# Linear attention scores from fp16 halves of phi, as 64-row products that alternate between row halves

## What is computed

```python
# layer 1, linear attention, per token s of each sequence b (16 heads of 64)
h = _ln(x, g1, beta1)
q = _phi((h @ wq).reshape(b, s, H, DH), proj)     # phi(y) = elu(y @ proj) + 1
k = _phi((h @ wk).reshape(b, s, H, DH), proj)
v = (h @ wv).reshape(b, s, H, DH)
kv = kv + k_t[..., :, None] * v_t[..., None, :]   # a running sum over the tokens
ksum = ksum + k_t
num = jnp.einsum('bhd,bhde->bhe', q_t, kv)
den = jnp.einsum('bhd,bhd->bh', q_t, ksum) + 1e-06
outs = num / den[..., None]
x = x + outs.reshape(b, s, H * DH) @ wo
x = x + (gelu(_ln(x, g2, beta2) @ w1 + b1) @ w2 + b2)
```

## Time and profile before

| | |
|---|---|
| median of 3 runs | 2643.98 us (2643.9 to 2645.58) |
| span of the profiled execution | 2644.0 us |
| layer 1 in it | about 0 to 853 us |
| first scores of group 0, 3 and 4 | 80.07, 276.90 and 375.74 us |
| PE, DVE, ACT, POOL busy share of the span | 93%, 71%, 60%, 26% |

### The profile page before, as it was taken

One profiled execution on the slowest core, in us unless ns is written; L12 is line 12 of the kernel. 1 busy time (PEld: TensorE's weight loads), 2 busy tenths in 40 slices (PEclk: granted clock), 3 DMA queues, 4 the chain that ended last, 5 costly groups with the idle time before them and its releaser, 6 DMA issues. The chain is left out here.

```text
span 2644.0 us, 61265 instructions
## 1 busy us (share of the span) xinstructions
PE 2451.5 (93%) x20194; PEld 1852.6 (70%) x20194; DVE 1877.7 (71%) x4914; ACT 1595.1 (60%) x3456; POOL 678.1 (26%) x1179
## 2 busy tenths in 40 slices
PE   5998998999996699999999999999999999979997
PEld 3775875875875467777777777777777777667886
DVE  5656656656654588778777887788777878656657
ACT  4335235235231578777777877787777778634444
POOL 1000100100101343434344443444343444200003
PEclk7999999999998799999999999999999999958999
DMA  4000000000000200000000000000000000022201
GB/s 127 27 1 1 0 0 0 0 0 0 0 1 5 86 14 9 13 8 13 8 13 8 13 8 13 8 13 8 13 7 12 8 7 0 2 65 77 92 24 56
DMA packets 45652, 50.08 MB, mean 19 GB/s; under 512 B 19120, under 2 KB 37664, under 8 KB 45504
## 3 DMA queue, kind: packets, MB, share of 16 engines
q1 hardware_dynamic: 45504, 48.45, 6.2%
HBM read 44.78 MB, written 3.67 MB: 18 GB/s over the span
## 5 line engine op out<-in xcount | busy, mean ns | idle before, releaser
L1390 POOL TENSOR_SCALAR p_norm<-p,p_rec 112x375 f32<-112x375 f32 x512 | 303.7, 593 | 831.6 <-DVE p_rec L1232 676.8
L1114 ACT ACTIVATE p<-s_neg,neg_max 112x375 f32<-112x375 f32 x512 | 309.8, 605 | 110.4 <-DVE neg_max L1227 88.0
L1236 DVE TENSOR_TENSOR pt_lo<-b_t,pt_hi 125x336 f16<-125x336 f32 x512 | 259.4, 507 | 158.4 <-ACT pt_hi L1120 148.1
L1212 DVE SCALAR_TENSOR_TENSOR k<-b_pb,k 64x375 f16<-64x375 f32 x512 | 280.9, 549 | 38.7 <-ACT k L1105 28.6
L1008 PE MATMUL b_t<-ident,p_norm 112*125 112x112 f32 x1536 | 283.1, 293 | 3.0 <-POOL p_norm L1390 3.0
L1105 ACT ACTIVATE k<-b_pb 64x375 f16<-64x375 f32 x512 | 244.9, 478 | 60.4 <-PE b_pb L64 53.8
L62 PE MATMUL b_o<-pt_hi,v_hi 125*64 125x112 f16 x1536 | 273.5, 221 | 6.2 <-DVE b_o_lo L1241 5.2
L1227 DVE CUSTOM_DVE_ANT_0 s_neg<-b_s,mask_bias 112x375 f32<-112x375 f32 x512 | 275.7, 539 | 0.6 <-ACT p L1114 0.4
L62 PEld LDWEIGHTS b_o<-pt_hi,v_hi 125*64 125x64 f16 x1536 | 167.5, 109 | 149.5 <-issue 103.0
L1120 ACT ACTIVATE pt_hi<-b_t 125x336 f16<-125x336 f32 x512 | 227.0, 443 | 61.5 <-PE b_t L1008 39.1
L63 PE MATMUL b_o<-pt_lo,v_hi 125*64 125x112 f16 x1536 | 261.3, 213 | 0.0
(11 more groups left out here) (247 smaller groups left out, 7003.8 us busy)
## 6 DMA issues: line engine op xcount, KB each, us to landing
w_raw<-in_L_ffn_W_dram SPq DMA_DIRECT2D x16, 1024.0 KB, 7.4
ctx<-in_ctx_dram SPq DMA_DIRECT2D x32, 375.0 KB
out_dram<-c_z SPq DMA_DIRECT2D x8, 448.0 KB, 3.2
x_sb<-in_x_dram SPq DMA_DIRECT2D x1, 3136.0 KB, 19.2
ff<-in_L_attn_w_dram SPq DMA_DIRECT2D x2, 1024.0 KB, 6.7
b_stage<-in_L_xattn_Wkv_dram SPq DMA_DIRECT2D x2, 1024.0 KB, 9.9
mask<-in_mask_BxS_bf_dram SPq DMA_DIRECT2D x32, 41.0 KB, 2.6
a_raw<-in_L_attn_wq_dram SPq DMA_DIRECT2D x1, 1024.0 KB, 5.0
```

Of the source, the lines that this page charges most:

```text
L1114: act.activation(p32[:, h % 4, :], s_neg[:, h % 2, :], ACT.Exp, bias=neg_max[:, h % 4:h % 4 + 1], scale=-1.0, accum_out=p_sum[:, h % 4:h % ...
L1212: ins = dve.scalar_tensor_tensor(k2[half_rows[1 - r], par, h, 0:S2], ps[rows, 0:S2], UNSCALE, k2[rows, par, h, 0:S2], ALU.mult, ALU.subtract)
L1236: dve.tensor_tensor(pt_lo[:, h % 4, :], t_ps[h % 2][0:JP, 0:JT * T], pt_hi[:, h % 4, :], ALU.subtract).then_inc(pt_lo_done, 1)
L1390: pool.tensor_scalar(p_norm[:, h % 4, :], p32[:, h % 4, :], p_rec[:, h % 4:h % 4 + 1], 0.0, ALU.mult, ALU.add).then_inc(p_norm_done, 1)
```

## The change

1. phi goes first to a ring of four fp32 tiles, `phi32`, by one 128-row VectorE operation for Q and K alike; VectorE then copies it to fp16 (`q_hi`, `k_hi`), and GpSimd subtracts to get the low half (`q_lo`, `k_lo`; new function `phi_low`). VectorE waits for its own first operation ahead of the copy, and for GpSimd's low half of four tiles before.
2. `kz`, its zeroes and the memset are gone.
3. `scores` forms two units at once, on even steps only: the even heads of four tiles go to `s_ps[0]` and the odd heads to `s_ps[1]`, three 64-row fp16 products for each head, in turn on rows 0 to 63 and 64 to 127. It waits for all masks before t.
4. `turn_output` makes four transposes on odd steps instead of two on each; `o32` interleaves the two units of a pair.

```diff
-        qt = sb("qt", [P, KI, GT], F32)
-        kz = sb("kz", [P, H, GT], F32)
+        NR = 4
+        phi32 = sb("phi32", [P, NR, GT], F32)
+        q_hi, q_lo, k_hi, k_lo = (sb(f"a_{n}", [P, KI, GT], F16) for n in ("q_hi", "q_lo", "k_hi", "k_lo"))
...
             def scores(g, u):
-                b, quad = divmod(u, 4)
-                at_least(pe, s_masked, UNITS * g + u - 1)
+
+                b, first = u // 4, 2 * (u % 4)
+                if b == 0:
+                    pe.wait_ge(qk_lo_done, tile_count(g, "K", first + 3) + 1)
+                at_least(pe, s_masked, UNITS * g + u)
+                cols = slice(b * T, (b + 1) * T)
                 for i in range(4):
-                    h = 4 * quad + i
-                    mm = pe.matmul(s_ps[u % 2][0:T, i * T:(i + 1) * T], kz[:, h, b * T:(b + 1) * T],
-                                   qt[:, h // 2, b * T:(b + 1) * T], start=True, stop=True)
-                mm.then_inc(s_ready, 1)
+                    for n, (k, q) in enumerate(((k_hi, q_hi), (k_lo, q_hi), (k_hi, q_lo))):
+                        for r in range(2):
+                            rows = slice(DH * r, DH * (r + 1))
+                            mm = pe.matmul(s_ps[r][0:T, i * T:(i + 1) * T], k[rows, first + i, cols], q[rows, first + i, cols],
+                                           start=(n == 0), stop=(n == 2))
+                            if i == 3 and n == 2:
+                                mm.then_inc(s_ready, 1)
...
             def turn_output(g, u):
                 pe.wait_ge(o_done, UNITS * g + u + 1)
-                ps = claim(use(g, "O", u // 2)) if u % 2 == 0 else bank(use(g, "O", u // 2))
-                for m in range(2):
-                    c = (2 * (u % 2) + m) * T
-                    mm = pe.transpose(ps[:, c:c + T], o32[:, u % 4, m * P:(m + 1) * P], ident[0:T, 0:T])
-                if u % 2 == 1:
-                    mm.then_inc(pb_ready, 1)
+                ps = claim(use(g, "O", u // 2))
+                for m in range(4):
+                    mm = pe.transpose(ps[:, m * T:(m + 1) * T], o32[:, u // 2 % 2, m * P:(m + 1) * P], ident[0:T, 0:T])
+                mm.then_inc(pb_ready, 1)
...
-                written(g, "K", KI)
                 written(g, "V", 2 * G4)
                 for t in range(STEPS):
-                    if t < UNITS:
+                    if t < UNITS and t % 2 == 0:
                         scores(g, t)
                     if VALUES_AT <= t < UNITS + VALUES_AT:
                         values(g, t - VALUES_AT)
-                    if TURN_AT <= t < UNITS + TURN_AT:
+                    if TURN_AT <= t < UNITS + TURN_AT and (t - TURN_AT) % 2 == 1:
                         turn_output(g, t - TURN_AT)
...
             def phi(g, kind, i):
...
-                if kind == "K":
-                    for r in range(2):
-                        rows = slice(DH * r, DH * (r + 1))
-                        ins = dve.scalar_tensor_tensor(kz[rows, 2 * i + r, :], ps[rows, 0:GT], 0.0, phi_exp[rows, i % 2, :],
-                                                       ALU.max, ALU.add)
-                else:
-                    ins = dve.scalar_tensor_tensor(qt[:, i, :], ps[:, 0:GT], 0.0, phi_exp[:, i % 2, :], ALU.max, ALU.add)
-                ins.then_inc(free_of(u), 1)
+                at_least(dve, qk_lo_done, n + 1 - NR)
+                dve.scalar_tensor_tensor(phi32[:, i % NR, :], bank(u)[:, 0:GT], 0.0, phi_exp[:, i % 2, :],
+                                         ALU.max, ALU.add).then_inc(free_of(u), 1)
+                dve.wait_ge(free_of(u), freed(u))
+                dve.tensor_copy(hi[:, i, :], phi32[:, i % NR, :]).then_inc(qk_hi_done, 1)
...
-            dve.wait_ge(kz_zeroed, 1)
...
+            def phi_low(g, kind, tiles):
+                hi, lo = (k_hi, k_lo) if kind == "K" else (q_hi, q_lo)
+                for i in tiles:
+                    settle(pool, passed, (qk_hi_done, tile_count(g, kind, i) + 1))
+                    pool.tensor_tensor(lo[:, i, :], phi32[:, i % NR, :], hi[:, i, :], ALU.subtract).then_inc(qk_lo_done, 1)
...
+                if not is_last(g):
+                    phi_low(g + 1, "Q", range(EARLY))
                 ln_rstd(g, 1)
+                if not is_last(g):
+                    phi_low(g + 1, "Q", range(EARLY, KI))
+                    phi_low(g + 1, "K", range(KI))
...
-            pool.memset(kz[:, :, :], 0.0).then_inc(kz_zeroed, 1)
...
+            for kind in ("Q", "K"):
+                phi_low(0, kind, range(KI))
```

More of the change, by code:

```diff
@@ L127, in layer1 @@
         rec = sb("rec", [T, 2, 4], F32)
-        o32 = sb("o32", [T, 4, 4 * DH], F32)
+        o32 = sb("o32", [T, 2, 8 * DH], F32)
         o_hi, o_lo = (sb(f"o_{n}", [P, 2, KI, T], F16) for n in ("hi", "lo"))
@@ L189, in use, with tile_count @@
             return g, len(PRE) + (LAST if is_last(g) else MAIN).index((kind, i))
+        def tile_count(g, kind, i):
+            return 2 * KI * g + (KI if kind == "K" else 0) + i
         def ready(u):
@@ L220, in layer1 @@
         h_hi_done = [sem(f"a_h_hi_done{i}") for i in range(2)]
-        kz_zeroed, pads_done = sem("a_kz_zeroed"), sem("a_pads_done")
+        qk_hi_done, qk_lo_done, pads_done = sem("a_qk_hi_done"), sem("a_qk_lo_done"), sem("a_pads_done")
         relu_done, exp_done = sem("a_relu_done"), sem("a_exp_done")
@@ L300, in values @@
                     mm = pe.matmul(o_ps[u % 2][0:T, i * (DH + 1):(i + 1) * (DH + 1)], sm[0:T + 1, u % NSM, i * T:(i + 1) * T],
-                                   v1[0:T + 1, b, 4 * quad + i, :], start=True, stop=True)
+                                   v1[0:T + 1, b, head(u, i), :], start=True, stop=True)
                 mm.then_inc(av_done, 1)
@@ L516, in divide @@
                     dve.wait_ge(pb_ready, ready(use(g, "O", u // 2 - 2)))
-                dve.tensor_tensor(o32[:, u % 4, :].rearrange("p (i d) -> p i d", d=DH), ps[:, :, 0:DH],
+                dve.tensor_tensor(o32[:, u // 2 % 2, :].rearrange("p (i r d) -> p i r d", r=2, d=DH)[:, :, u % 2, :], ps[:, :, 0:DH],
                                   rec[:, u % 2, :].unsqueeze(2).to_broadcast([T, 4, DH]), ALU.mult).then_inc(o_done, 1)
```

9 lines of the change are left out of this document (6 added, 3 removed).

## The result

The changed kernel takes 2800.07 us (median of four runs, 2796.03 to 2801.91) against 2644.03 beside it: a ratio of 1.0588, 95% interval 1.0575 to 1.0601. The forecast was 2682, the range 2634 to 2728. The sign was right; the size, 38 us for 156, was not.

A forecast was written before the change was run, and what follows sets the result against it. PE, busy 93% of the span and never pausing in the attention loop, was taken as the bound. 2644.0 + 56 (pairing's wait) - 14 (behind the loop) - 4 (ahead of group 0) = 2682 us, range 2634 to 2728.

The forecast's parts named there:

- S: PE time of a pair's 24 fp16 scores products in the attention loop: 1.2 us, 0.37 less than before.
- rival 1: Both row halves' scores products stream together, S = 0.6: 2648 us, no measurable change; chance 0.22.
- The wait that comes with pairing: Attention loop: a pair's scores wait for the last mask of the pair before; +7.0 us a group, +56 in all.
- my formula: A pair's cycle in the loop: S + 2.86 us, + 0.53 with `o_lo`, + 0.33 for each small even-step operation.
- point (b): PE idle 1.5 to 2 us ahead of each pair's scores, masks waiting for `a_o`; about 35 us to unit 14.
- The loop's end: End of a group's attention loop: as before, fewer transposes being no gain.
- Point (e): PE clock 1.00 in the attention loop; 0.50 would show the clock falling there.
- rival 3: The clock falls in the attention loop, four 3.4 us stretches a group at half clock: +48, sum 2730; chance 0.10.
- layers 2 and 3 start when layer 1 ends: Listed among the other edits, which cost nothing: the layers behind layer 1 add no time.
- phi and the stretch behind the loop: Copies beside POOL's subtractions, 1.35 us a tile, and sums moved off `xh`: -2 us a group, -14 over seven.
- rival 2: The stretch behind the loop gains 5.4 us a group, with the row halves together: 2624 us; chance 0.10.
- Ahead of group 0: `kz` memsets no longer delay `xh`, eight Q tiles take back 1.6: -4 us, bounds -6 and 0.

The follow-up runs named there:

- the unpaired kernel: Changed kernel with each unit's scores issued in its own step as twelve products of one row half, waiting for the mask of two units before: 2780.41 us.
- unpaired, written-out kernel: Changed kernel with scores unpaired and DVE's groups 1 to 6 of layer 1 written out in place of a loop: 2753.47 us.
- filler run: Changed kernel with five fp16 products of 448 columns added ahead of each pair's scores, overwritten by them: 2766.96 us.
- The four buffers: Changed kernel with four buffers for masked scores (sm) instead of two, pairing kept: 2746.15 us.
- 28 waits: Kernel before with 28 long-satisfied waits added in DVE's loop of layer 1, at a group's end: 2653.59 us beside 2641.3.
- moved loops: Changed kernel with satisfied waits added once ahead of layer 1's loop, 170 on DVE and 240 on PE, no loop altered: 2782.12 us.
- the run with the sums later: Kernel before with one more wait: POOL's two sums of a group wait for DVE's four xh of the second layer norm: 2599.9 us.
- run without low halves: Changed kernel with POOL's subtraction of the low halves replaced by a memset of two columns from group 1 on: 2749.28 us.
- fillers and four buffers: Changed kernel, still paired, with four sm buffers, DVE's groups written out and five 448-column products ahead of each pair's scores: 2728.02 us.

## Why the prediction missed

Step by step, in the order in which it put them.

*S.* Taken as 1.2 us a pair, measured 0.61: the forecast took the serial pace, and rival 1 (both halves stream at once) was right. With it my sum would have been 2648, further off and no measurable change, so that the sign came out right owes something to a wrong S. The Trainium skill ("TensorE: Matmul & The Clock Gate", Part 3) has products on different row groups of the array run at the same time. The trace agrees: 24 that alternate take 0.61 us, and so do 12 of one half in the unpaired kernel. The Trainium skill's "TensorEngine Tiling (Array Packing)", Key Properties, has TensorE drained at a change of tiling mode. The trace has a pause at both changes that fits it, but a small one. A step of the unpaired, written-out kernel at full clock:

```profile
292.33 0.25 PE L302 MATMUL a_s<-a_q_hi,a_k_hi 64*112 64x112 f16 x1 [0.45 <-DVE sm L514]
...
292.94 0.21 PE L302 MATMUL a_s<-a_q_lo,a_k_hi 64*112 64x112 f16 x1
293.08 1.00 PE L315 MATMUL a_o<-v,sm 113*112 113x65 f32 x8
294.01 0.25 PE L302 MATMUL a_s<-a_q_hi,a_k_hi 64*112 64x112 f16 x1
```

From the last score to the first value 0.14 pass, where scores are 0.05 apart; from the first value to the next scores 0.93, where eight values took 0.75. Two changes cost some 0.09 + 0.18 us a step, my estimate from these rows, which is more than the 0.12 that the shorter scores save (12 x 0.055 = 0.66 for 0.78).

*The wait that comes with pairing.* The mechanism was right, and its size nearly, at full clock. A pair with `o_lo` and two small operations, worked by my formula with S = 0.61, is 4.7 us; at full clock it took 4.9 (456.01 to 460.90). The masks wait for `a_o`, as point (b) said. The prediction measured from a group's first scores to those of unit 14: 224.9 us in sum before, 350.7 after, +126 where I had +56. The filler run's groups at full clock take 34.2 for it; with the fillers' own 1.0 off each of the two pairs with a W and 0.2 off the first, that is 32.0 against 28.3 before. So pairing at full clock costs 3.7 a group, 30 in sum, by this estimate; my figure for S = 0.6 was 22. The four buffers confirm the term by removing it. The loop's end is as before, as I wrote: from the scores of unit 14 to the last values 6.5 us in a middle group of either kernel. The table's third row grew by 16 only because a pair's last scores now come earlier in it.

*The clock.* This is the step that failed. Point (e) expected 1.00 in the loop; rival 3 had the clock fall, for 3.4 us at a time because the pause in the earlier trace rows had cost that much, and priced it at +48 with a chance of 0.10. It fell within 4 us of a group's first scores (8 in group 0) and stayed down for 17 to 27 us, and it fell again for 3 to 7 us further on. Of the 126 us, 20 are the stall at DVE's branch and 30 pairing; the 76 that are left are the clock's. The filler run bears this out: its 75 us less are the stall and the clock, with some 17 us of the fillers' own and 4 of half clock still in its loops. The error was to carry a duration over from other work: the earlier trace rows show a pause followed by full-height fp16 products, and the loop has 64-row ones and fp32 values of 65 columns. The kernel before ran at 1.00 there with PE busy throughout, and no row said what other products would do to it; the groups of the unpaired, written-out kernel that fell with no pause above 0.45 us show that with fp16 scores no long pause is needed.

*Code placement.* Not in the prediction at all. I had costed instructions by their time on the engine only. Longer programs on DVE and PE moved loops to places where instructions are fetched anew in every iteration. That is 20 us at DVE's branch in layer 1, and +12 behind layer 1's last values, 10.5 of it in layer 2's iterations, which I had put at nothing ("layers 2 and 3 start when layer 1 ends"). By the runs with 28 waits and with moved loops the 12 go with DVE's place, not with PE's. The order of instructions doesn't show it, and no row of before has it.

*phi and the stretch behind the loop.* Forecast -2 a group, measured +3.2. The two parts were seen: the sums no longer ahead of `xh` (by the run with the sums later worth 5.6 a group, against 5.4 in rival 2, which is what the rows added up to), and copies held by POOL's subtractions (forecast 1.35 a tile, measured 1.47). The mis-sized term is the second, 7.4 us a group by the run without low halves. I added up only the pace of six tiles; `h_lo` and `xh` meet the subtractions too, and the MLP's first copies meet the sums, where I took 1 us lost. Nor did I have the second 3.4 us at half clock that this stretch now has, worth up to 1.7. PE's waits there (total, times, longest):

```profile
PE a_pb L62 <- DVE phi L506: 3.7, 4, 2.4
PE a_pb L62 <- DVE ff L612: 3.3, 2, 1.8
```

*Ahead of group 0.* Forecast -4, measured -5.3 (first scores at 74.75): right, as far as can be told. The same stretch differs by 3 us between kernels that have the same code there (76.8 to 80.1 in those without the change).

The sum with its causes: 30 (pairing) + 20 (DVE's branch) + 76 (clock) to the scores of unit 14, 1 at the loop's end, 22 behind the loop, -5 and 12 make the 156 us. The clock's share is what the other two leave, and the 30 are an estimate, so the two can be off against each other by some us.

No version with fp16 scores came out ahead of the kernel before. At full clock their loop takes 31.3 us unpaired, with PE busy all but 0.45 us, and 31.1 at best paired, with fillers and four buffers, against 30.7 in a middle group before: the changes between row heights eat what the products save, and pairs, which have half as many, make PE wait for DVE. The best kernel of this study is the kernel before with its sums moved, 2599.9 us.

What stays open: how the clock's fall is decided within a group. Two groups with the same products differed, and these runs show only that more work for PE prevents it, in all groups when given at the start, in most when given in PE's waits. Which places of a loop are bad is also not derived here, only that such places exist.

## What to carry to other kernels

Ask of an edit what it does to the clock, not only to the busy time: cheaper products on TensorE can cost more by the clock than they save, and a few full products in idle time can pay for themselves several times over. When a loop's code grows or moves, read the page's instruction packets and the `issue` idle behind each branch first, in layers that weren't touched as well. And keep POOL's long operations away from DVE's with both ends in SBUF: one wait that put them beside DVE work from PSUM gave 1.6%.

## What the hardware showed that was not expected

- A branch back to a loop's head takes 0.2 to 0.3 us, or 3.3 to 4.0 us (DVE and PE), up to 5.2 in layer 2 of the filler run, depending on where the loop lies in the engine's program; moving it by some 85 and 120 instructions removed it.
- Layer 2, unchanged, took 88.6, 89.7 or 93.2 us an iteration (medians) by what stands ahead of it in DVE's and PE's programs.
- TensorE at half clock and busy for 23.80 of 23.80 us did not regain the full clock with 64-row fp16 scores and 65-column fp32 values among them. Eight products of 448 columns a group kept it at 1.00.
- Twelve 64-row products of one row half take 0.61 us, and twenty-four that alternate between the halves, into two banks, 0.61 too.
- A loop whose groups fall to half clock or not is also a loop whose runs scatter: 16 to 18 us between runs of the unpaired kernels, 0.8 between the two runs of the kernel whose clock held. That one comes of the other is not shown.
